# A hybrid network's second layer: ternary weights made by VectorE in pieces, squares added in pairs, and another interleaving of two half-sequences

## The chip, the cores and the metric

One Trainium2 chip, one of its cores. A core has TensorE (PE, matrix products; PEld is its weight load), VectorE (DVE), ScalarE (ACT), GpSimd (POOL) and SyncE (SP, which issues the transfers here). Each engine works through its own instructions in program order; engines wait for each other on semaphores. The metric is the device time of one execution in microseconds (us), less is better. Times in the text are us unless marked.

## The reference, cut to what matters

The network has two layers on a sequence of 1024 tokens with 256 features. The first (attention with rope, a routed block, attention with biases, the routed block again) is not touched. The second is:

```
x = x + L1_attn_a(layernorm(x))     # "r": gates, values = split(h @ W + b); sigmoid, tanh; h_t = g_t * h_(t-1) + v_t
x = x + L1_ffn(layernorm(x))        # "t1": silu(h @ wu) * (h @ wg) @ wd, with ternary weights
x = x + L1_attn_b(layernorm(x))     # "l", "n2", "m": see below
x = x + L1_ffn(layernorm(x))        # "t2": the same ternary weights

def ternary_quant(w):               # 256 x 1024 each
    scale = mean(abs(w)) + 1e-8
    return clip(round(w / scale), -1, 1) * scale

def L1_attn_b(x):
    xn = rmsnorm(x, norm1_w)
    left = gelu(xn @ left_W + left_b)
    right = rg_lru(causal_conv4(xn @ right_W + right_b), ...)   # two gates, exp, sqrt, a scan over the sequence
    x1 = left * right @ out_W + out_b + x
    x1n = rmsnorm(x1, norm2_w)
    return gelu(x1n @ up1_W + up1_b) * (x1n @ up2_W + up2_b) @ down_W + down_b + x1
```

A norm needs for each token the mean over the 256 features and the mean of the squares of what is left after the mean is taken off.

## The kernel before, in words

Features lie on the partitions: x is [128, 2, 1024], two tiles of 128 features (KT = 2) by 1024 tokens. Nearly every product is made of fp32r parts: an operand is split into a rounded "hi" and the rest "lo", and hi·hi, lo·hi and hi·lo are added up in PSUM. A ternary weight needs no lo part, so a block of `up` or `gate` is four matmuls of 128x512 (two hi, two lo), and one step of `down` is four as well; `right`, `left`, `ga`, `gx`, `out`, `up1`, `up2` take six.

The second layer runs in one stage (`layer1`, L1309). The sequence is cut in two halves of 512 tokens, half 0 and half 1, each with four PSUM banks and its own buffers; the second needs the first's last column in the two scans and the convolution. For each engine there are three programs: one that prepares weights (`prep_*`) and one for each half (`half_*`). `by_turns` runs each of them up to its next `yield`, in the order that a string of digits says: 0 for prep, 1 for half 0, 2 for half 1. The four strings (`L1_PE`, `L1_DVE`, `L1_ACT`, `L1_POOL`) are written out, so each engine's order is fixed; when the string is used up, what is left of the programs follows one after the other.

What the prediction speaks of:

- **Norm of a half.** TensorE multiplies x by a constant matrix for the mean (L1552); VectorE subtracts (L1594); ScalarE squares, tile by tile (L1573); TensorE forms the mean of squares as one-column products, four groups of 128 tokens by two tiles (L1562), each an fp32 product that the trace shows as two passes; ScalarE takes the root (L1580); VectorE inverts it and puts it on a diagonal (L1606, L1600); TensorE spreads it over the partitions (L1566); VectorE scales (L1630), ScalarE makes hi (L1587), VectorE lo (L1615). There are ten such variances: r, t1, l, n2, t2 for each half.
- **Ternary weights.** ScalarE sums the absolute values (L1472), TensorE averages over partitions (L1453), VectorE forms the scale and the two bounds (L1506 to L1509), and GpSimd makes the weights in three whole-tensor instructions of 128x2048 for each of up, gate and down: below (L1523), above in place (L1526), above minus below (L1529). After them GpSimd splits the other eight weights into hi and lo (L1540, L1542).
- **The ternary block, t1 and t2.** For f = 0 to 7: up block, sigmoid (L1770), silu on VectorE (L1842), gate block, product (L1846), hi on ScalarE (L1763), lo on GpSimd (L1968), and two steps later the down block (L1661, L1664). The first up, gate and down wait for GpSimd's weights. At the end VectorE adds the result to x (L1850).
- **The l part** adds x1 to u (L1929) when `out` is done; the m part, six steps of f, ends with L1947.
- **r** ends with a scan (L1824) and the sum into x (L1827), VectorE's, for each feature tile.

## Time and profile before

| | |
|---|---|
| median of 3 runs | 1779.75 us (1777.93 to 1782.86) |
| profiled execution | 1778.83 us, of which its span is 1777.6 |
| second layer within the span | 1471 to 1776: 305 us |
| PE busy in those 305 us | 254.2 us, mean granted clock 0.89 |
| DVE / ACT / POOL busy in them | 179.6 / 152.7 / 142.1 us |

In the span, 0 is the start of the profiled program. A timeline row reads: start, duration, engine, line, operation, what it writes and reads, shapes, how many were merged, and in brackets the idle time of the engine just before and what ended it. PEclk, the granted clock, is a share of full speed (2.4 GHz; the lower level is 1.2 GHz, and a stretch between 0.5 and 1 has had both).

### The profile page before, as it was taken

What the parts mean: (1) busy time and instruction counts of PE and PEld (TensorE: products, weight loads), DVE (VectorE), ACT (ScalarE), POOL (GpSimd) and SP (SyncE); (2) the same over time, 40 slices, a digit from 0 to 9 for tenths busy, and PEclk for the clock granted to TensorE, in tenths of its full rate; (3) what the DMA queues carried; (4) which work ended last, traced back from release to release, by engine and by line L of the source; (5) the groups of instructions that cost most, each with busy time, mean ns of one, the idle gap of its engine ahead of it and who ended that gap; (6) DMA issues with size and microseconds to landing.
All of it is one profiled execution on the core that took longest, in us unless ns stands there. A gap on an engine that the chain in (4) does not pass through costs nothing.

```text
span 1777.6 us, 24716 instructions
## 1 busy us (share of the span) xinstructions
PE 1526.5 (86%) x8394; PEld 1259.6 (71%) x8394; DVE 1194.1 (67%) x2825; ACT 966.2 (54%) x2119; POOL 694.4 (39%) x777
## 2 busy tenths in 40 slices
PE   6889897989888887677699999999996777787898
PEld 4768686777777776367488888888884664565676
DVE  4788788888888886453466666666665536577445
ACT  2676767677776776122265555555551235344654
POOL 4446363645545443310242433243322204871223
PEclk8899999999999999787899999999997888898899
DMA  1000000000000000500100000000005004000000
GB/s 65 10 10 7 10 16 1 16 1 16 1 7 1 7 1 1 237 1 0 42 19 13 25 17 20 13 25 19 7 1 237 1 1 166 0 0 1 1 1 24
DMA packets 13936, 46.23 MB, mean 26 GB/s; under 512 B 3058, under 2 KB 3058, under 8 KB 11380
## 3 DMA queue, kind: packets, MB, share of 16 engines
q1 hardware_dynamic: 13812, 44.66, 7.0%
q8 instruction: 68, 1.11, 0.3%
q14 instruction: 56, 0.46, 0.1%
HBM read 43.60 MB, written 1.05 MB: 25 GB/s over the span
## 4 chain that ended last, share of the span: by engine, by line
PE 59%; DVE 18%; ACT 12%; issue 7%; POOL 3%; DMA 0%; DVEq 0%; ACTq 0%; POOLq 0%; SPq 0%
PE ps L140 22%; PE ps L343 13%; PE ps L332 6%; ACT a_prob L362 4%; DVE a_pT_lo L403 4%; PE ps L1651 2%; PE ps L1645 2%; ACT a_pT_hi L395 2%; DVE a_prob L354 2%; ACT a_q L579 1%; PE ps L1155 1%; PE ps L1088 1%; PE ps L213 1%; PE ps L1647 1%; DVE f_r L1283 1%
## 5 line engine op out<-in xcount | busy, mean ns | idle before, releaser
L378 POOL TENSOR_SCALAR a_prob<-a_prob,a_rowinv 128x128 f32<-128x128 f32 (+7 forms) x256 | 192.2, 752 | 307.8 <-DVE a_rowinv L371 307.7
L362 ACT ACTIVATE a_prob<-a_prob,a_negmax 128x128 f32<-128x128 f32 (+7 forms) x256 | 199.0, 777 | 73.8 <-DVE a_negmax L354 72.8
L403 DVE TENSOR_TENSOR a_pT_lo<-ps,a_pT_hi 128x512 fp32r<-128x512 f32 (+3 forms) x384 | 200.9, 551 | 24.4 <-ACT a_pT_hi L395 22.0
L332 PE MATMUL ps<-ident,a_prob 128*128 128x128 f32 x1152 | 177.4, 283 | 41.3 <-DVE a_pT_lo L403 37.0
L378 POOL TENSOR_SCALAR b_prob<-b_prob,b_rowinv 128x128 f32<-128x128 f32 (+7 forms) x128 | 96.2, 751 | 260.6 <-DVE b_rowinv L371 260.6
L354 DVE CUSTOM_DVE_ANT_0 a_prob<-ps,a_mask 128x128 f32<-128x128 f32 (+7 forms) x256 | 191.5, 748 | 2.4 <-PE ps L140 2.3
L395 ACT ACTIVATE a_pT_hi<-ps 128x512 fp32r<-128x512 f32 (+3 forms) x384 | 173.6, 487 | 32.9 <-PE ps L332 29.7
L332 PEld LDWEIGHTS ps<-ident,a_prob 128*128 128x128 f32 x1152 | 135.6, 144 | 65.2 <-POOL a_prob L378 31.7
L140 PE MATMUL ps<-a_k_hi,a_q 128*128 128x512 f32 (+3 forms) x384 | 156.0, 406 | 4.1 <-DVE a_k_lo L628 1.4
L343 PE MATMUL ps<-a_pT_hi,a_v 128*128 128x512 f32 (+3 forms) x384 | 132.3, 352 | 19.5 <-DVE a_pT_lo L403 19.0
L140 PE MATMUL ps<-a_k_lo,a_q 128*128 128x512 f32 (+3 forms) x384 | 131.6, 355 | 0.0
L343 PE MATMUL ps<-a_pT_lo,a_v 128*128 128x512 f32 (+3 forms) x384 | 124.6, 348 | 0.0
L403 DVE TENSOR_TENSOR b_pT_lo<-ps,b_pT_hi 128x128 fp32r<-128x128 f32 (+2 forms) x192 | 99.9, 548 | 2.2 <-ACT b_pT_hi L395 1.5
L362 ACT ACTIVATE b_prob<-b_prob,b_negmax 128x128 f32<-128x128 f32 (+7 forms) x128 | 100.1, 782 | 2.0 <-DVE b_negmax L354 2.0
L343 PEld LDWEIGHTS ps<-a_pT_hi,a_v 128*128 128x128 f32 x384 | 73.1, 190 | 39.5 <-issue 15.9
L1968 POOL TENSOR_TENSOR l_ring_lo<-l_work,l_ring_hi 128x512 fp32r<-128x512 f32 x44 | 57.3, 1307 | 103.8 <-ACT l_ring_hi L1763 103.6
L354 DVE CUSTOM_DVE_ANT_0 b_prob<-ps,b_mask 128x128 f32<-128x128 f32 (+7 forms) x128 | 95.8, 749 | 0.6 <-PE ps L140 0.6
L395 ACT ACTIVATE b_pT_hi<-ps 128x128 fp32r<-128x128 f32 (+2 forms) x192 | 86.3, 488 | 15.0 <-PE ps L332 15.0
L140 PEld LDWEIGHTS ps<-a_k_hi,a_q 128*128 128x128 f32 x384 | 76.3, 199 | 19.6 <-DVE a_negmax L354 11.4
L332 PE MATMUL ps<-ident,b_prob 128*128 128x128 f32 x576 | 84.1, 273 | 2.2 <-POOL b_prob L378 1.7
L636 DVE TENSOR_TENSOR a_o_sum<-ps,a_o_low 64x512 f32<-64x512 f32 x64 | 43.8, 684 | 58.9 <-ACT a_o_low L587 57.9
L140 PEld LDWEIGHTS ps<-a_k_lo,a_q 128*128 128x128 f32 x384 | 76.0, 198 | 6.0
(436 smaller groups left out, 4187.3 us busy)
## 6 DMA issues: line engine op xcount, KB each, us to landing
f_wq<-in_f_wq SPq DMA_DIRECT2D x2, 2048.0 KB, 9.9
f_wo<-in_f_wo SPq DMA_DIRECT2D x2, 2048.0 KB, 18.6
b_w_raw<-in_b_qk SPq DMA_DIRECT2D x16, 256.0 KB, 2.7
a_w_raw<-in_a_w SPq DMA_DIRECT2D x8, 384.0 KB, 3.1
a_o_raw<-in_a_o SPq DMA_DIRECT2D x8, 256.0 KB, 2.6
f_rope<-in_f_rope SPq DMA_DIRECT2D x2, 1024.0 KB, 5.3
f_wk<-in_f_wk SPq DMA_DIRECT2D x2, 1024.0 KB, 11.7
f_wv<-in_f_wv SPq DMA_DIRECT2D x2, 1024.0 KB, 14.4
```

The lines of the kernel that those rows point to most:

```text
L140: t = pe.matmul(out, a, b, start=start and n == 0, stop=stop and n == len(passes) - 1, skip_group_check=True)
L332: t = pe.transpose(g.ps[:, b, j * P:j * P + P], a.prob[:, slot, (j0 + j) * P:(j0 + j + 1) * P], g.ident[:])
L343: t = pe.matmul(out[:, q:HALF], x, y, start=(j == 0 and n == 0), stop=(j == tiles - 1 and n == len(passes) - 1), skip_group_check=True)
L354: dve.tensor_tensor_reduce(a.prob[:, slot, 0:width], g.ps_flat[:, bank * HALF:bank * HALF + width], a.mask[:, N - width:], -1.0, -MASKED, ...
L362: act.activation(prob, prob, ACT.Exp, bias=a.negmax[:, slot:slot + 1], scale=-1.0, accum_out=a.rowsum[:, slot:slot + 1]).then_inc(*g.exped ...
L378: pool.tensor_scalar(prob, prob, a.rowinv[:, slot:slot + 1], 1.0, ALU.mult, ALU.mult).then_inc(*g.normed.mark(a.tag, u))
L395: act.activation(hi, src, ACT.Copy).then_inc(*g.hi.mark(a.tag, u, j0 // 4))
L403: dve.tensor_tensor(lo, src, fr(hi), ALU.subtract).then_inc(*g.lo.mark(a.tag, u, j0 // 4))
L636: dve.tensor_tensor(a.o_sum[ROWS[h % 2], qb], out[0:64], a.o_low[64:128], ALU.add).then_inc(*g.drained.mark(*ev))
L1645: pe.matmul(out, hi[:, k, mm], q.hi[:, k], start=k == 0, stop=False, skip_group_check=True)
L1651: t = pe.matmul(out, hi[:, k, mm], q.lo[:, k], start=False, stop=k == KT - 1, skip_group_check=True)
L1968: pool.tensor_tensor(q.ring_lo[:, f % RING], q.hid[:, f % RING], fr(q.ring_hi[:, f % RING]), ALU.subtract).then_inc(*q.pool.mark(tag, "lo" ...
```

## The change

Three things, all in the second layer.

1. The ternary weights are made by VectorE, in pieces of 1024 columns, two pieces for each weight and two instructions for each piece: below by `tensor_scalar`, then `(raw > bound) - below` in one `scalar_tensor_tensor`. The pieces stand in `prep_dve`, and their places among VectorE's other work are set by the string. GpSimd's three instructions for each weight are gone.
2. ScalarE's two squared tiles are added by VectorE (`half_squares_dve`), and the one-column products are taken over the sum: 4 instead of 8 instructions for a norm. TensorE waits for VectorE there instead of ScalarE. Beside it, the last lo part of each t1, m and t2 is made by VectorE (`half_last_dve`) instead of GpSimd.
3. All four strings are new.

```
-L1_PE = '12121201121211221201...'
+L1_PE = '12121201122101102212...'
 (L1_DVE, L1_ACT and L1_POOL are replaced in the same way)
...
@@ prep_dve
-    for n in range(3):
+    for n, (name, _, _) in enumerate(TERNARY):
...
+        raw, w = l.raw["t", name][:].rearrange(FLAT), l.tern[name][:].rearrange(FLAT)
+        for c in range(2):
+            cc = slice(c * T_E, c * T_E + T_E)
+            dve.wait_ge(*done.at("bounds", n))
+            dve.tensor_scalar(l.below[:, cc], raw[:, cc], s[:, 2:3], None, ALU.is_lt).then_inc(*done.mark("below", n, c))
+            yield
+            dve.wait_ge(*done.at("below", n, c))
+            dve.scalar_tensor_tensor(w[:, cc], raw[:, cc], s[:, 1:2], l.below[:, cc], ALU.is_gt,
+                                     ALU.subtract).then_inc(*done.mark("t", name, c))
+            yield
@@ prep_pool
-    for n, (name, _, _) in enumerate(TERNARY):
-        raw, w = l.raw["t", name][:].rearrange(FLAT), l.tern[name][:].rearrange(FLAT)
...
-        pool.tensor_scalar(l.below[:], raw, l.scale[:, n, 2:3], None, ALU.is_lt).then_inc(*done.mark("below", n))
...
-        pool.tensor_scalar(raw, raw, l.scale[:, n, 1:2], None, ALU.is_gt).then_inc(*done.mark("above", n))
...
-        pool.tensor_tensor(w, raw, l.below[:], ALU.subtract).then_inc(*done.mark("t", name))
-        yield
@@ half_scale_pe
-    pe.wait_ge(*q.act.at(tag, "sq", KT - 1))
+    pe.wait_ge(*q.dve.at(tag, "squares"))
     for j in range(HT):
-        for k in range(KT):
-            t = pe.matmul(q.bank[1][:, j:j + 1], q.sq[:, k, j * P:j * P + P], g.avg[:, 0:1], start=k == 0, stop=k == KT - 1)
+        t = pe.matmul(q.bank[1][:, j:j + 1], q.sq[:, 0, j * P:j * P + P], g.avg[:, 0:1], start=True, stop=True)
+def half_squares_dve(dve, q, tag):
+    dve.wait_ge(*q.act.at(tag, "sq", KT - 1))
+    dve.tensor_tensor(q.sq[:, 0], q.sq[:, 0], q.sq[:, 1], ALU.add).then_inc(*q.dve.mark(tag, "squares"))
+    yield
@@ half_down
-    pe.wait_ge(*q.pool.at(tag, "lo", f))
+    pe.wait_ge(*(q.dve if f == count - 1 else q.pool).at(tag, "ring_lo", f))
@@ half_ternary_pe (and the same for gate and down)
-                pe.wait_ge(*g.prep_pool.at("t", "up"))
+                pe.wait_ge(*g.prep_dve.at("t", "up", 1))
+def half_last_dve(dve, q, tag, f):
+
+    dve.wait_ge(*q.act.at(tag, "ring", f))
+    dve.tensor_tensor(q.ring_lo[:, f % RING], q.hid[:, f % RING], fr(q.ring_hi[:, f % RING]),
+                      ALU.subtract).then_inc(*q.dve.mark(tag, "ring_lo", f))
```

`half_squares_dve` is called in each norm after the mean is taken off (for n2 after x1), `half_last_dve` before the last additions to x; `half_hidden_pool` runs over `count - 1` steps.

How the instructions move is told at three places. In the rows, `half0_act` and the like are semaphores of one half and engine, `prep_*` those of the weights' programs.

First VectorE, before, from the scale of `up` to the centring of half 0 in t1: the lo parts of half 1, the scans and sums of r (L1824, L1827).

```order
L1506 TENSOR_SCALAR l_scale<-ps 128x1 [waits prep_pe]
L1508 TENSOR_SCALAR l_scale<-l_scale 128x1 [waits prep_dve]
L1509 TENSOR_SCALAR l_scale<-l_scale 128x1
L1615 TENSOR_TENSOR l_h_lo<-l_h,l_h_hi 128x512 [waits half1_act] x2
L1824 SCALAR_TENSOR_TENSOR l_left<-l_work 128x512 [waits half0_act]
L1827 TENSOR_TENSOR x<-x,l_left 128x512 [waits half0_dve]
L1829 COPY l_r_last<-l_left 128x1
L1824 SCALAR_TENSOR_TENSOR l_left<-l_work,l_r_last 128x512 [waits half1_act,half0_dve]
L1827 TENSOR_TENSOR x<-x,l_left 128x512 [waits half1_dve]
L1824 SCALAR_TENSOR_TENSOR l_left<-l_work 128x512 [waits half0_act]
```

The same place of the change (L1515 and L1518 are the pieces, L1827 and L1830 scan and sum):

```order
L1515 TENSOR_SCALAR l_below<-l_t_raw_up,l_scale 128x1024 [waits prep_dve]
L1518 SCALAR_TENSOR_TENSOR l_t_up<-l_t_raw_up,l_scale,l_below 128x1024 [waits prep_dve]
L1515 TENSOR_SCALAR l_below<-l_t_raw_up,l_scale 128x1024 [waits prep_dve]
L1827 SCALAR_TENSOR_TENSOR l_left<-l_work 128x512 [waits half0_act]
L1830 TENSOR_TENSOR x<-x,l_left 128x512 [waits half0_dve]
L1832 COPY l_r_last<-l_left 128x1
L1518 SCALAR_TENSOR_TENSOR l_t_up<-l_t_raw_up,l_scale,l_below 128x1024 [waits prep_dve]
L1506 TENSOR_SCALAR l_scale<-ps 128x1 [waits prep_pe]
L1508 TENSOR_SCALAR l_scale<-l_scale 128x1 [waits prep_dve]
L1509 TENSOR_SCALAR l_scale<-l_scale 128x1
L1515 TENSOR_SCALAR l_below<-l_t_raw_gate,l_scale 128x1024 [waits prep_dve]
L1827 SCALAR_TENSOR_TENSOR l_left<-l_work 128x512 [waits half0_act]
```

Pieces of the weights now stand between the scans of half 0, and half 0's second scan comes ahead of half 1's first.

Second TensorE at the start of t1, before: the first blocks of up and gate of the two halves stand in turn.

```order
L1645 MATMUL ps<-l_h_hi,l_t_up 128x512 [waits half0_act,prep_pool]
L1645 MATMUL ps<-l_h_hi,l_t_up 128x512 [waits half0_act]
L1651 MATMUL ps<-l_h_lo,l_t_up 128x512 [waits half0_dve] x2
L1566 MATMUL ps<-l_diag,ones 128x512 [waits half1_dve]
L1645 MATMUL ps<-l_h_hi,l_t_up 128x512 [waits half1_act,prep_pool]
L1645 MATMUL ps<-l_h_hi,l_t_up 128x512 [waits half1_act]
L1651 MATMUL ps<-l_h_lo,l_t_up 128x512 [waits half1_dve] x2
L1645 MATMUL ps<-l_h_hi,l_t_gate 128x512 [waits prep_pool]
```

And in the change (L1648 and L1654 are the hi and lo products, L1558 the one-column ones):

```order
L1648 MATMUL ps<-l_h_hi,l_t_up 128x512 [waits half0_act,prep_dve]
L1648 MATMUL ps<-l_h_hi,l_t_up 128x512 [waits half0_act]
L1654 MATMUL ps<-l_h_lo,l_t_up 128x512 [waits half0_dve] x2
L1558 MATMUL ps<-avg,l_sq 128x1 [waits half1_dve]
L1558 MATMUL ps<-avg,l_sq 128x1 x3
L1648 MATMUL ps<-l_h_hi,l_t_gate 128x512 [waits prep_dve]
L1648 MATMUL ps<-l_h_hi,l_t_gate 128x512
L1654 MATMUL ps<-l_h_lo,l_t_gate 128x512 x2
L1648 MATMUL ps<-l_h_hi,l_t_up 128x512 [waits half0_dve]
```

Half 0 goes ahead alone there: half 1's first up block comes after half 0's second down block. When TensorE has issued half 0's last down block of t1, 84 of half 1's 96 matmuls of t1 are still to come; before it was 56.

Third GpSimd after the split of r's weights, as one piece of the difference (L1537 and L1539 are L1540 and L1542 of before):

```order
-L1523 TENSOR_SCALAR l_below<-l_t_raw_up,l_scale 128x2048
-L1526 TENSOR_SCALAR l_t_raw_up<-l_t_raw_up,l_scale 128x2048
-L1529 TENSOR_TENSOR l_t_up<-l_t_raw_up,l_below 128x2048
-L1523 TENSOR_SCALAR l_below<-l_t_raw_gate,l_scale 128x2048
-L1526 TENSOR_SCALAR l_t_raw_gate<-l_t_raw_gate,l_scale 128x2048
-L1529 TENSOR_TENSOR l_t_gate<-l_t_raw_gate,l_below 128x2048
-L1523 TENSOR_SCALAR l_below<-l_t_raw_down,l_scale 128x2048
-L1526 TENSOR_SCALAR l_t_raw_down<-l_t_raw_down,l_scale 128x2048
-L1968 TENSOR_TENSOR l_ring_lo<-l_work,l_ring_hi 128x512
-L1529 TENSOR_TENSOR l_t_down<-l_t_raw_down,l_below 128x2048
```

The splits of left, right and ga follow r's at once, ahead of the first lo part of half 0.

## Rows read from the trace of the kernel before

**Rows 1.** The page: the span, and busy time of each engine.
```profile
span 1777.6 us, 24716 instructions
PE 1526.5 (86%) x8394; PEld 1259.6 (71%) x8394; DVE 1194.1 (67%) x2825; ACT 966.2 (54%) x2119; POOL 694.4 (39%) x777
```
**Rows 2.** Stretches of the second layer: length, busy time of each engine, granted clock, DMA.
```profile
1495.00:1515.00 20.00, 10.20 (x36) 6.42 (x35) 14.16 (x11) 6.53 (x9) 9.49 (x2) 0.74 0.00 1
1515.00:1532.00 17.00, 10.19 (x35) 5.55 (x34) 10.07 (x20) 6.61 (x10) 15.80 (x4) 0.74 0.00 0
1532.00:1547.50 15.50, 11.59 (x40) 8.56 (x38) 7.33 (x10) 6.21 (x10) 15.41 (x5) 0.83 0.00 0
...
sum 305.00, PE 254.16 PEld 184.56 DVE 179.56 ACT 152.71 POOL 142.12; mean PE 23.11 PEld 16.78 DVE 16.32 ACT 13.88 POOL 12.92
```
**Rows 3.** Waits of PE from 1471 to 1776: us in total, times, longest.
```profile
PE ps L1552 <- DVE l_r_last L1829: 9.5, 1, 9.5
PE ps L1661 <- POOL l_t_down L1529: 3.5, 1, 3.5
PE ps L1645 <- POOL l_t_gate L1529: 3.3, 1, 3.3
```
**Rows 4.** Timeline of POOL: the ternary weights, and a later split.
```profile
1487.65 6.32 POOL L1523 TENSOR_SCALAR l_below<-l_t_raw_up,l_scale 128x2048 bf16<-128x2048 f32 x1 [8.85 <-DVE l_scale L1509]
1494.07 5.44 POOL L1526 TENSOR_SCALAR l_t_raw_up<-l_t_raw_up,l_scale 128x2048 f32<-128x2048 f32 x1
1499.60 4.97 POOL L1529 TENSOR_TENSOR l_t_up<-l_t_raw_up,l_below 128x2048 fp32r<-128x2048 f32 x1
...
1543.34 4.07 POOL L1529 TENSOR_TENSOR l_t_down<-l_t_raw_down,l_below 128x2048 fp32r<-128x2048 f32 x1
...
1579.34 3.45 POOL L1542 TENSOR_TENSOR l_up_lo<-l_raw_up,l_up_hi 128x1536 fp32r<-128x1536 f32 x1
```
**Rows 5.** Timeline of DVE beside those POOL instructions.
```profile
1494.21 4.65 DVE L1824 TENSOR_TENSOR_SCAN l_left<-l_work,l_r_last 128x512 f32<-128x512 f32 x1
...
1499.51 1.22 DVE L1824 TENSOR_TENSOR_SCAN l_left<-l_work 128x512 f32<-128x512 f32 x1
1500.76 4.36 DVE L1827 TENSOR_TENSOR x<-x,l_left 128x512 f32<-128x512 f32 x1
...
1580.03 2.77 DVE L1867 TENSOR_TENSOR l_inv<-l_inv 128x4 f32<-128x4 f32 x1
```
**Rows 6.** DVE's groups by form: busy time, mean ns of one.
```profile
L1248 DVE TENSOR_TENSOR f_diag<-f_s,ident 128x1024 f32<-128x1024 f32 x2 | 2.5, 1226 | 0.1
...
L1908 DVE SCALAR_TENSOR_TENSOR l_work<-l_work,l_right 128x512 f32<-128x512 f32 x4 | 2.8, 694 | 0.1
...
L1051 DVE TENSOR_SCALAR f_probT<-f_s,f_s_col 128x896 bf16<-128x896 f32 x2 | 1.3, 674 | 0.0
```
**Rows 7.** Timeline of PE at full clock: a block, and the one-column products of a norm.
```profile
1736.24 1.84 PE L1562 MATMUL ps<-avg,l_sq 128*128 128x1 f32 x16
1737.94 0.71 PE L1645 MATMUL ps<-l_h_hi,l_t_gate 128*128 128x512 f32 x2
...
1765.04 0.62 PE L1645 MATMUL ps<-l_h_hi,l_t_up 128*128 128x512 f32 x2
1765.50 0.63 PE L1651 MATMUL ps<-l_h_lo,l_t_up 128*128 128x512 f32 x2
1765.97 0.63 PE L1645 MATMUL ps<-l_h_hi,l_t_gate 128*128 128x512 f32 x2
```
**Rows 8.** Timeline of DVE: the additions that end t1, l and m.
```profile
1569.26 1.41 DVE L1850 SCALAR_TENSOR_TENSOR x<-ps,l_scale,x 128x512 f32<-128x512 f32 x2 [1.52 <-PE ps L1664]
...
1610.96 1.41 DVE L1850 SCALAR_TENSOR_TENSOR x<-ps,l_scale,x 128x512 f32<-128x512 f32 x2 [7.53 <-PE ps L1664]
...
1628.16 0.75 DVE L1929 SCALAR_TENSOR_TENSOR l_u<-ps,l_bias,l_u 128x512 f32<-128x512 f32 x1 [1.81 <-PE ps L1651]
...
1685.73 0.75 DVE L1929 SCALAR_TENSOR_TENSOR l_u<-ps,l_bias,l_u 128x512 f32<-128x512 f32 x1 [1.81 <-PE ps L1651]
1687.08 1.56 DVE L1947 SCALAR_TENSOR_TENSOR x<-ps,l_bias,x 128x512 f32<-128x512 f32 x2 [0.60 <-PE ps L1664]
```
**Rows 9.** The chain of waits at the end: start, duration, what.
```profile
1767.70 0.76 DVE l_work L1846
...
1770.51 0.76 DVE l_work L1846
1771.27 0.02 issue
1771.29 0.64 ACT l_ring_hi L1763
1771.94 0.07 issue
1772.01 1.27 POOL l_ring_lo L1968
1773.28 0.04 issue
```

More of the change, by code:

```diff
@@ L1344 @@
 HT = HALF // P
[L1345 to L1348 removed]
+L1_PE = '1212120112210110221211211121111112112111111111211121222122222111221111111222222221122121121112212221212222111111112212112122122122222222221122112121111211121111211122122121222222221212222222222'
+L1_DVE = '10121202012112112202000100012110012012211110200112001121122211111122111112112111222211121111111111112221122111111112211212212211112122212222222222221221222212222222112112221211212111222111212112121122211211222211222222122122122122122222'
+L1_ACT = '1120201201122110121201212121121211112112211111121112211222121211111112112111221212112111221112121221122222212222121212212211222112122121222222211211111221121112212122212222122222222'
+L1_POOL = '0000100110112112022212121011211212122222211111212212222'
 def by_turns(g, e, order, *programs):
@@ L1517, in prep_pool @@
     yield
-    for n, (name, _, _) in enumerate(TERNARY):
-        raw, w = l.raw["t", name][:].rearrange(FLAT), l.tern[name][:].rearrange(FLAT)
-        pool.wait_ge(*g.prep_dve.at("bounds", n))
-        if n:
-            pool.wait_ge(*done.at("t", TERNARY[n - 1][0]))
-        pool.tensor_scalar(l.below[:], raw, l.scale[:, n, 2:3], None, ALU.is_lt).then_inc(*done.mark("below", n))
-        yield
-        pool.wait_ge(*done.at("below", n))
-        pool.tensor_scalar(raw, raw, l.scale[:, n, 1:2], None, ALU.is_gt).then_inc(*done.mark("above", n))
-        yield
-        pool.wait_ge(*done.at("above", n))
-        pool.tensor_tensor(w, raw, l.below[:], ALU.subtract).then_inc(*done.mark("t", name))
-        yield
     for name, _, _ in L_W:
@@ L1626, in half_norm_dve @@
     yield from half_centre_dve(dve, q, tag)
+    yield from half_squares_dve(dve, q, tag)
     yield from half_inverse_dve(g, dve, q, tag)
@@ L1696, in half_ternary_pe @@
             if f == 0:
-                pe.wait_ge(*g.prep_pool.at("t", "gate"))
+                pe.wait_ge(*g.prep_dve.at("t", "gate", 1))
             else:
@@ L1703, in half_ternary_pe @@
             if f == 2:
-                pe.wait_ge(*g.prep_pool.at("t", "down"))
+                pe.wait_ge(*g.prep_dve.at("t", "down", 1))
             half_down(pe, q, down, f - 2, TE_T, tag)
@@ L1847, in half_ternary_dve @@
         yield
+    half_last_dve(dve, q, tag, TE_T - 1)
+    yield
     for m in range(KT):
@@ L1856, in half_lru_dve @@
     yield from half_centre_dve(dve, q, "l")
+    yield from half_squares_dve(dve, q, "l")
     dve.wait_ge(*act.at("l", "std"))
@@ L1930, in half_lru_dve @@
         yield
+    yield from half_squares_dve(dve, q, "n2")
     yield from half_inverse_dve(g, dve, q, "n2")
@@ L1943, in half_lru_dve @@
         yield
+    half_last_dve(dve, q, "m", RF_T - 1)
+    yield
     for m in range(KT):
@@ L1965, in half_hidden_pool @@
 def half_hidden_pool(pool, q, tag, count):
-    for f in range(count):
+    for f in range(count - 1):
         pool.wait_ge(*q.act.at(tag, "ring", f))
         pool.tensor_tensor(q.ring_lo[:, f % RING], q.hid[:, f % RING], fr(q.ring_hi[:, f % RING]),
-                           ALU.subtract).then_inc(*q.pool.mark(tag, "lo", f))
+                           ALU.subtract).then_inc(*q.pool.mark(tag, "ring_lo", f))
         yield
```

4 lines of the change are left out of this document (removed).

## The prediction

> **What bounds the kernel now.** I read the page first: 1777.6 us of span, PE busy 86% of it [rows 1]. The change touches the second layer alone, so next the stretches of that layer: 305 us, in which PE is busy 254.2 us, DVE 179.6 and POOL 142.1 [rows 2]. PE is the busiest engine there, but 51 us it stands idle, and much of its busy time is at a reduced clock. Three stretches in a row are the poorest: from 1495 to 1547.5 PE is busy 10.2 of 20, 10.2 of 17 and 11.6 of 15.5 us, at granted clocks of 0.74, 0.74 and 0.83, which lie between its two levels, 1.2 and 2.4 GHz [rows 2]. In the last two of them POOL is busy 15.8 of 17 and 15.4 of 15.5 us [rows 2]: there POOL is the bound. The waits of PE say on what: 9.5 us on VectorE's end of r (L1829), 3.5 and 3.3 us on POOL's ternary weights for down and gate [rows 3]. The timeline of POOL shows the chain: 6.32, 5.44 and 4.97 us for up, and so on until the last of nine, for down, ends at 1543.34 + 4.07 = 1547.4 [rows 4].
>
> The 9.5 us wait on VectorE has the same root. A scan of 128x512 takes 1.22 us when nothing disturbs it, but the one that begins at 1494.21, just behind POOL's L1526 at 1494.07, takes 4.65; and the sum L1827, which begins at 1500.76 under POOL's L1529 (1499.60 + 4.97 = 1504.57), takes 4.36 and ends at 1505.12 [rows 4, 5]. An instruction over 512 columns with two inputs in SBUF takes 0.69 when free [rows 6]. So VectorE lost 3.4 + 3.7 = 7.1 us there to POOL, on the path of half 0 into t1.
>
> This is what the Trainium skill says in SBUF — State Buffer, "SBUF: two separate sides": VectorE and GpSimd share a pair of ports as an exclusive lock, and an instruction of VectorE with two SBUF inputs waits for the whole instruction of GpSimd that came first. This trace agrees in the main: L1827 ends 0.55 us behind POOL's L1529 and L1867 with POOL's L1542, but the scan ended 0.65 us before L1526 did [rows 4, 5].
>
> **The change part by part.**
>
> *Ternary weights.* Removed: POOL's nine instructions, 6.32 + 5.44 + 4.97 for up and about 15 each for the others, some 46 us [rows 4]. Added on VectorE: six pieces. Below is a one-input compare to bf16; the same form over 896 columns takes 0.674 [rows 6], so 0.77 at 1024. The other has two SBUF inputs; the nearest row is a tensor_tensor over 1024 columns, 1.226 [rows 6], and L1908 shows that the scalar form costs no more than the plain one. A piece is 2.0 us, six are 12.0. Bounds: 4 us less if the bf16 input sped up the second instruction to the first one's rate (6 times 0.46 makes 2.8), and 12 us more if each of the six met a POOL split: the long one takes 3.45 [rows 4], half of it waited for is 1.7, and 0.3 for each piece's hand-overs comes to it. I take 12.0, as most splits are short.
>
> Now I walk the start with these durations. VectorE's work for the r norm comes some 2 us later than before, since the second half's add waits for ScalarE behind the softplus; so the scale of up is known at about 1489 and up's first piece ends at 1491.5. The scans then stand between pieces: half 0's first at 1493 to 1494.2, its second, behind up's second piece and gate's first compare, ends at 1498.6, the sum at 1499.2. That was 1505.1. Mean, centring, squares, add, one-column products, root, diagonal and its product (the same steps as before, with one gate piece in the way) bring the first up block of half 0 to about 1512.5; before it was 1519.5. Gate's weights are complete at 1508, so its first gate block follows at once, where it was held until 1531.0. From there half 0 runs alone, limited by its own chain. The end of the trace gives the period of such a chain: L1846 of one f begins at 1767.70, that of the next at 1770.51, 2.81 apart [rows 9]. At the lower clock and with the down pieces and half 1's norm on VectorE's queue (4.0 + 0.9 + 2.7 us) the first two steps take 4.5 each, the other six 3.0 to 3.3. Its last addition to x comes at about 1547; it was at 1569.26 + 1.41 = 1570.7 [rows 8]. That is 24 us for half 0.
>
> *But half 1 pays for part of it.* When half 0 ends t1, 84 matmuls of half 1's t1 are left instead of 56. A block of four takes 1765.97 − 1765.04 = 0.93 us at full clock, 0.233 for each matmul [rows 7]. So I take the next landmark where both orders have done the same: half 0's residual of m (L1947, ends 1687.08 + 1.56 = 1688.6 [rows 8]), with half 1's x1 just before it.
> By the road of TensorE: before, from 1570.7 to 1688.6 are 118 us, in which 284 matmuls (66 us) and 14.7 us of norm products fall (two means, four variances, six inverses, near 1.7, 1.7 and 0.9 each; the 1.70 is from row L1562 to the next start [rows 7]); 37 us are lost. In the change 312 matmuls are 73 us, the norms 11.3; with the same loss that is 121, so 1668.
> By the road of half 1's chain: half 0 goes from the end of t1 (1570.7) to its x1 (1628.16 + 0.75 = 1628.9) in 58.2 us [rows 8]. In it L1867, over 4 columns, took 2.77 under POOL's 3.45 of L1542 [rows 4, 5], and the instructions after it met the next splits: about 4 us that go, since most splits are now made earlier. So x1 of half 0 at 1601, and half 1's end of t1, which stands just behind it, at 1606 (before 1612.4). From there half 1 took 1686.5 − 1612.4 = 74.1 us to its x1; half 0 took 58.2. That gives 1664 to 1680.
> I take 1668, where the first road ends and within the second: 20.4 us less than 1688.6.
>
> *Squares in pairs.* Each norm saves half of 1.70 us on TensorE, 0.85, and adds a 128x512 add with two SBUF inputs, 0.69 [rows 6], and a hand-over of some 0.05. Where the norm is on the path that nets 0.1; where TensorE is the bound it is 0.85. Four variances are in the walk, four in the sum above (3.4 us), two come after it: 1.7 us, in a stretch where PE is full. Bounds: nothing, or 0.85 each.
>
> *The last lo part.* At the end of the kernel POOL's 1.27 us is on the chain [rows 9]; VectorE's is 0.69. That is 0.6 us. Elsewhere other blocks hide it.
>
> *The strings.* After the landmark the order is nearly what it was; ScalarE changes its table three more times in the layer, and I give that nothing, because half of the stretch is PE-bound.
>
> Sum: 20.4 + 1.7 + 0.6 = 22.7 us off the profiled execution's 1778.8, so 1756. The median of before, 1779.75, is 0.9 above that execution; I forecast 1757.
>
> **The rivals.**
>
> *Half 1's chain decides* (13 in 100). Its l part takes the full 74.1 us again, since half 0's m part now runs wholly beside it. For: half 0's x1, behind which m begins, comes 5 us before half 1 enters l, where it came 16.5 us after [rows 8]. Against: TensorE has the room. Landmark at 1680: 6.5 + 2.3 off, 1770.
>
> *TensorE's idle time shrinks as well* (15 in 100). Half 0's l part has 84 matmuls of half 1 beside it, 6.6 us more, and where PE idles less its clock stays up: the stretches above at 0.74 would have been a quarter shorter. If 10 of the 37 lost us go too, 1746.
>
> *The lock moves with the weights* (6 in 100). POOL's splits of left, right, ga, gx, out and up1 now run beside VectorE's pieces, scans and adds, all of two SBUF inputs, and half 0's lo parts queue behind a split of 5 us. If the pieces pay the 12 us upper bound and each of them is ahead of a silu, half 0 ends t1 at 1560 and the landmark is near 1679: 1768. By the skill's rule this would happen wherever the two start together; POOL has 46 us less to hold the lock with, which is why I give it little.
>
> *Slower: half 1 comes too late* (3 in 100). Before, after half 0's t1, half 1's last four steps of f took 1612.4 − 1570.7 = 41.7 us, 10.4 each, stretched by half 0's l part. If seven steps are stretched so, half 1 ends t1 at 1547 + 73 = 1620, 8 us later than before, and everything behind it too: 1785 to 1788. It decides from 1612.4 plus the 5 us of a measurable loss. Against it: the last steps stand close behind half 0's x1.
>
> *The walk is right but the saved time is given back* (4 in 100), for instance by the mean of half 1, which waits on its scan ahead of half 0's inverse: within 5 us of 1779.75.
>
> **How the numbers follow.** The forecast has 59 in 100, with a range of its own from 1749 to 1765: the two roads' ends. Half 1's chain, more room and the lock bring it to 1741 and 1771, which leaves out the two last cases and a little on the fast side. A difference of 0.3%, 5.3 us, is about what a measurement of this kernel tells from no change. Faster by more than that: 0.59 + 0.13 + 0.15 + 0.06 = 0.93; the same 0.04; slower 0.03.
>
> **What would show it right or wrong.** Right: six instructions of 0.75 and six of 1.23 us on VectorE, no waits of PE on ternary weights; half 0's end of t1 near 1547, x1 of half 1 near 1667, the end of the layer near 1753; DVE scans of r at 1.22. The rule of the pieces is wrong if they take 3 us or more. The whole is wrong if the end of half 0's t1 is early and half 1's x1 not: then the gain was only moved from one half to the other. If PE's busy time falls by more than the 8.5 us of the one-column products, the clock gave it.

## The result, and the profile after

| | median, us | ratio to before, 95% interval |
|---|---|---|
| before | 1778.84 | 1 |
| changed | 1757.84 (1756.06 to 1758.47) | 0.9878 [0.9858, 0.9899] |

The forecast was 1757. The page of the changed kernel, first its length and then the busy times:

```profile
span 1756.0 us, 24570 instructions
PE 1514.6 (86%) x8314; PEld 1248.7 (71%) x8314; DVE 1213.1 (69%) x2853; ACT 968.6 (55%) x2122; POOL 645.1 (37%) x762
```

Against [rows 1] TensorE has 11.9 us less to do, and yet the span fell by 21.6: TensorE also stood idle for 9.7 us less. The waits of TensorE in the second layer, over 2 us (total, times, longest):

```profile
PE ps L1558 <- DVE l_sq L1596: 10.0, 6, 3.7
PE ps L1648 <- ACT l_h_hi L1583: 9.4, 9, 1.9
PE ps L1648 <- DVE l_work L1845: 5.4, 3, 3.3
PE ps L1648 <- ACT l_work L1814: 3.4, 4, 2.5
PE ps L1549 <- DVE l_r_last L1832: 3.1, 1, 3.1
PE ps L1562 <- DVE l_diag L1602: 2.9, 3, 1.4
```

No ternary weight is waited for any more; L1549's 3.1 answers to the 9.5 of [rows 3]. In place of these waits, TensorE now waits 10.0 us for VectorE's new additions of squares, L1596. The landmarks on VectorE's timeline (start, duration): half 0 ends t1, half 1 ends t1, half 1's x1 (L1942), half 0 ends m, half 1 ends t2.

```profile
1549.23 1.41 DVE L1855 SCALAR_TENSOR_TENSOR x<-ps,l_scale,x 128x512 f32<-128x512 f32 x2 [0.17 <-PE ps L1667]
...
1607.55 1.40 DVE L1855 SCALAR_TENSOR_TENSOR x<-ps,l_scale,x 128x512 f32<-128x512 f32 x2
...
1663.17 0.75 DVE L1942 SCALAR_TENSOR_TENSOR l_u<-ps,l_bias,l_u 128x512 f32<-128x512 f32 x1 [0.66 <-PE ps L1654]
...
1670.65 1.44 DVE L1963 SCALAR_TENSOR_TENSOR x<-ps,l_bias,x 128x512 f32<-128x512 f32 x2 [1.14 <-PE ps L1667]
...
1752.52 1.41 DVE L1855 SCALAR_TENSOR_TENSOR x<-ps,l_scale,x 128x512 f32<-128x512 f32 x2 [0.83 <-PE ps L1667]
```

The ends of these (1550.6, 1609.0, 1663.9, 1672.1 and 1753.9) answer to 1570.7, 1612.4, 1686.5 and 1688.6 in [rows 8] and to 1775.5 at the end of the kernel before:

```profile
1774.09 1.41 DVE L1850 SCALAR_TENSOR_TENSOR x<-ps,l_scale,x 128x512 f32<-128x512 f32 x2 [2.83 <-PE ps L1664]
```

Half 0's t1 gained 20.1 us, half 1's only 3.4, half 1's x1 22.6, half 0's m (the landmark of the prediction) 16.5, and the end 21.6.

### The profile page after: what moved, and what is told of

Same layout as the page of the kernel before. It is cut to its first block, busy times and chain, and to the rows that moved or that the text cites. A ratio compares the mean times of both kernels' runs of the same rounds, so it can differ in the third digit from the quotient of the medians.

```text
span 1756.0 us, 24570 instructions
## 1 busy us (share of the span) xinstructions
PE 1514.6 (86%) x8314; PEld 1248.7 (71%) x8314; DVE 1213.1 (69%) x2853; ACT 968.6 (55%) x2122; POOL 645.1 (37%) x762
## 4 chain that ended last, share of the span: by engine, by line
PE 59%; DVE 19%; ACT 13%; issue 7%; POOL 1%; DMA 0%; DVEq 0%; ACTq 0%; POOLq 0%; SPq 0%
PE ps L140 22%; PE ps L343 13%; PE ps L332 6%; ACT a_prob L362 4%; DVE a_pT_lo L403 4%; ACT a_pT_hi L395 2%; PE ps L1648 2%; PE ps L1654 2%; DVE a_prob L354 2%; ACT a_q L579 1%; PE ps L1155 1%; PE ps L1088 1%; PE ps L213 1%; DVE f_r L1283 1%; DVE a_q L626 1%
## 5 line engine op out<-in xcount | busy, mean ns | idle before, releaser
L343 PE MATMUL ps<-a_pT_hi,a_v 128*128 128x512 f32 (+3 forms) x384 | 132.2, 351 | 19.4 <-DVE a_pT_lo L403 19.0
L343 PE MATMUL ps<-a_pT_lo,a_v 128*128 128x512 f32 (+3 forms) x384 | 124.7, 348 | 0.0
L1984 POOL TENSOR_TENSOR l_ring_lo<-l_work,l_ring_hi 128x512 fp32r<-128x512 f32 x38 | 49.6, 1314 | 138.3 <-ACT l_ring_hi L1766 138.3
L140 PEld LDWEIGHTS ps<-a_k_hi,a_q 128*128 128x128 f32 x384 | 76.3, 199 | 19.6 <-DVE a_negmax L354 11.5
## 6 DMA issues: line engine op xcount, KB each, us to landing
f_wk<-in_f_wk SPq DMA_DIRECT2D x2, 1024.0 KB, 11.9
```

The costliest lines, as they stand in the source:

```text
L140: t = pe.matmul(out, a, b, start=start and n == 0, stop=stop and n == len(passes) - 1, skip_group_check=True)
L343: t = pe.matmul(out[:, q:HALF], x, y, start=(j == 0 and n == 0), stop=(j == tiles - 1 and n == len(passes) - 1), skip_group_check=True)
L1984: pool.tensor_tensor(q.ring_lo[:, f % RING], q.hid[:, f % RING], fr(q.ring_hi[:, f % RING]), ALU.subtract).then_inc(*q.pool.mark(tag, "rin ...
```

## The layer in four stretches

The table below is what the experiments are read by. It is worked out from the timeline of each profiled execution, counted from the first matmul of the second layer (L1549 or L1552). That is needed because the first layer, the same in all kernels, did not end at the same time. A row is one execution, each figure rounded by itself; the ratios are those of all runs. Of two kernels, with the pieces alone and with the last third interleaved anew, these are the starts:

```profile
1475.15 3.67 PE L1549 MATMUL ps<-x,avg 128*128 128x512 f32 x8 [0.83 <-PE ps L1170]
```

```profile
1468.54 3.67 PE L1549 MATMUL ps<-x,avg 128*128 128x512 f32 x8 [0.83 <-PE ps L1170]
```

They lie 6.6 us apart, more than most effects here. So a landmark's time on the clock can't be compared between two executions, unless both layers start together, as those of before and of the changed kernel do (1471.1).

| kernel | to t1 end, half 0 | to t1 end, half 1 | to m end, half 0 | to the end | layer | ratio of times |
|---|---|---|---|---|---|---|
| before | 99.6 | 41.7 | 76.3 | 86.9 | 304.4 | 1 |
| pieces alone | 93.4 | 41.5 | 76.0 | 86.8 | 297.8 | 0.9959 [0.9938, 0.9981] |
| new rows alone | 91.3 | 61.9 | 60.9 | 82.5 | 296.6 | 0.9959 [0.9944, 0.9973] |
| pieces + new rows | 80.9 | 55.6 | 60.9 | 82.5 | 279.9 | 0.9869 [0.9849, 0.9890] |
| changed (those + pairs) | 79.5 | 58.3 | 63.1 | 81.8 | 282.8 | 0.9878 [0.9858, 0.9899] |
| new rows + pairs, no pieces | 92.6 | 65.7 | 62.8 | 81.8 | 302.9 | 0.9982 [0.9970, 0.9994] |
| changed, another first norm | 80.6 | 56.4 | 59.9 | 81.8 | 278.8 | 0.9865 [0.9850, 0.9880] |
| the same without pairs | 78.3 | 56.9 | 62.8 | 82.4 | 280.4 | 0.9882 [0.9868, 0.9896] |
| the same, pairs in the last two norms | 78.2 | 55.1 | 60.4 | 81.8 | 275.6 | 0.9853 [0.9835, 0.9871] |

## Experiments: the parts one by one

"New rows" are the interleaving of the changed kernel, with the last lower half on VectorE.

**The pieces alone.** Before, with

```
+ (prep_dve, behind each scale)  is_lt to bf16, then is_gt and subtract, 2 x 128x1024
- (prep_pool)                    below, above, t: 3 x 128x2048 for each weight
  VectorE's row: four steps of 0 behind each scale; the other rows as before
```

> The kernel before, with one part of the change: VectorE makes the ternary weights in pieces of 128x1024, each of the three sets right behind its scale; GpSimd no longer makes them. Sums of squares, last lower half and interleaving stay as before (the three scales' places in VectorE's row too). Theory A (the gain is that the first up block and the first down block of half 0 stop waiting for GpSimd, and that the half that waited 24 us less then starts everything earlier): the first up block starts near 1512 where it was 1519.5, the 3.5 and 3.3 us waits of TensorE for ternary weights are gone, half 0 ends t1 near 1555 or earlier where it was 1570.7; the interleaving of before holds part back, so about 1764 us, 1757 to 1771. Rival B (the new interleaving carries the gain, the weights' engine is a side matter): over 1774. Rival C (fewer one-column products carry it): over 1774 too.

It took 1775.99 us (1767.29 to 1777.16) against 1781.36 of before, ratio 0.9959. Theory A asked for 1757 to 1771 and fell; rivals B and C both asked for this number, and the next runs tell them apart. The waits for ternary weights did go, but only 6.2 us in the first stretch came of it. TensorE's timeline shows what came next:

```profile
1516.91 0.28 PE L1453 MATMUL ps<-l_part,l_avg 128*128 128x1 f32 x2
1522.56 3.57 PE L1559 MATMUL ps<-avg,l_sq 128*128 128x1 f32 x16 [5.37 <-ACT l_sq L1570]
1525.99 1.20 PE L1642 MATMUL ps<-l_h_hi,l_t_up 128*128 128x512 f32 x2
```

L1559 are half 1's one-column products, which stand in TensorE's row ahead of half 0's first up block (L1642). They wait 5.37 us for half 1's squares. VectorE shows why:

```profile
1516.59 0.76 DVE L1515 TENSOR_SCALAR l_below<-l_t_raw_gate,l_scale 128x1024 bf16<-128x1024 f32 x1
1517.38 1.28 DVE L1518 SCALAR_TENSOR_TENSOR l_t_gate<-l_t_raw_gate,l_scale,l_below 128x1024 fp32r<-128x1024 f32 x1
...
1519.36 1.28 DVE L1518 SCALAR_TENSOR_TENSOR l_t_gate<-l_t_raw_gate,l_scale,l_below 128x1024 fp32r<-128x1024 f32 x1
1520.56 1.28 DVE L1591 TENSOR_TENSOR l_h<-x,ps 128x512 f32<-128x512 f32 x2
```

Gate's four instructions run ahead of half 1's centring (L1591). The up weights are there, but the row lets half 0 go no faster than half 1: its first up block comes 50.8 us into the layer, where before it came at 48.4. The pieces stood right behind each scale here; other places for them in the old rows were not tried, so the 6.2 us hold for these places.

**The new rows alone.** The changed rows of TensorE, ScalarE and VectorE, with the weights on GpSimd and 8 products:

```
- dve: pieces, squares          + pool: below, above, t (nine steps)
  GpSimd's row: '0000000001011001102110202020212121...'
```

> The new interleaving alone: ternary weights on GpSimd as before (GpSimd's splits between the lower halves again), 8 one-column products, no additions of squares; TensorE's, ScalarE's and VectorE's rows are the new ones, with the last lower half on VectorE. It completes the square of which before (1780.8 in the last call), the pieces alone (1776.0) and pieces with rows (1757.65) are three corners. Theory (early weights and rows that let half 0 run ahead are worth little apart and 20 us together, since TensorE then neither waits for weights nor for half 1): 1776 us, 1772 to 1780. Rival (they add up): 1781 less 18, 1763. With the additions of squares this corner took 1777.7.

1771.32 us against 1779.13, ratio 0.9959. So apart each part is worth 0.41%; if they multiplied, both would give 0.9918, and they give 0.9869. The missing 0.5% is some 9 us (give or take 6, by the three intervals) that neither has without the other. The theory has the sign and the kind right, though the rows alone did better than the 1776 expected and fell just under its range. In the first stretch the pieces are worth 6.2 us under the old rows and 10.4 under the new ones; 6.3 more come in the second.

**The changed kernel with the weights back on GpSimd.**

```
- dve: pieces    + pool: below, above, t    (additions of squares stay)
```

> The changed kernel, with the ternary weights back on GpSimd in the three whole passes each of before; GpSimd's row begins as before (its splits of left, right, ga, gx, out and the others between the lower halves again), VectorE's row is that of the changed kernel without the pieces. Squares in pairs, the last lower half on VectorE and the interleaving of TensorE, VectorE and ScalarE stay as changed. Theory A: the gain is lost, and an order made for early weights sits on late ones: the first up block near 1519, TensorE's waits for ternary weights back; 1778 us, 1770 to 1788. Rival B (the interleaving carries the gain): under 1764. If the parts add up: 1757.8 plus what the pieces alone gained.

1777.71 us, ratio 0.9982 [0.9970, 0.9994]: theory A's number and not rival B's, nor the 1763 of parts that add up. TensorE waits for the weights again:

```profile
PE ps L1561 <- DVE l_sq L1599: 12.7, 6, 3.2
...
PE ps L1667 <- POOL l_t_down L1529: 5.8, 1, 5.8
PE ps L1552 <- DVE x L1833: 4.4, 1, 4.4
```

**The changed kernel without the pairs.**

```
-    pe.wait_ge(*q.dve.at(tag, "squares"))            (4 products)
+    pe.wait_ge(*q.act.at(tag, "sq", KT - 1))         (8 products)
-    yield from half_squares_dve(...)                 in r, t1, l, n2, t2
```

> The changed kernel, with 8 one-column products in each norm again and without VectorE's ten additions; all else as changed. Theory A: TensorE's busy time up by about 8.5 us, of which what is saved on VectorE takes back nearly all up to the landmark at 1672 and not behind it, where half 1 alone feeds TensorE: 1759.5 us, 1757 to 1762. Rival C (the squares carry a good part of the gain): 1766 or more. Rival (the additions only cost): 1754 or less.

1757.65 us against the changed kernel's 1757.84, so no worth of the pairs as placed in it can be told. Theory A had this, within its range. The cause shows in two groups of the changed kernel (busy time and mean ns of one, then the idle time ahead):

```profile
L1558 PE MATMUL ps<-avg,l_sq 128*128 128x1 f32 x80 | 12.8, 281 | 10.2 <-DVE l_sq L1596 10.0
```

```profile
L1596 DVE TENSOR_TENSOR l_sq<-l_sq 128x512 f32<-128x512 f32 x10 | 10.9, 1092 | 3.4 <-ACT l_sq L1569 3.4
```

Before had 160 of these products in 19.4 us with 6.7 us of waits ahead of them; now 80 take 12.8 with 10.0. The busy time saved is 6.6 us, the waits are 3.3 longer, and an addition takes 1.09 us on average where I had written 0.69. The worst one:

```profile
1601.75 1.49 POOL L1537 TENSOR_SCALAR l_down_hi<-l_raw_down 128x1536 fp32r<-128x1536 f32 x1
1603.32 3.76 POOL L1539 TENSOR_TENSOR l_down_lo<-l_raw_down,l_down_hi 128x1536 fp32r<-128x1536 f32 x1
```

```profile
1603.70 3.93 DVE L1596 TENSOR_TENSOR l_sq<-l_sq 128x512 f32<-128x512 f32 x1
1607.55 1.40 DVE L1855 SCALAR_TENSOR_TENSOR x<-ps,l_scale,x 128x512 f32<-128x512 f32 x2
```

Half 0's addition begins 0.38 us behind GpSimd's lower half of down, and ends 0.55 behind its end; half 1's end of t1 stands behind it. That is the 58.3 against 55.6 us of the second stretch in this execution. This is again the exclusive lock of the Trainium skill's page SBUF — State Buffer, "SBUF: two separate sides", and here the trace agrees.

## Experiments: where an addition stands

**Before, with the pairs alone.**

```
+ half_squares_dve in every norm, 4 products
  VectorE's row: a step ahead of each reciprocal or of what needs TensorE behind the products
```

> The kernel before, with one part of the change: VectorE adds the two blocks of squares, and TensorE does 4 one-column products in a norm instead of 8. Everything else as before; the ten additions are put into VectorE's row ahead of whatever needs TensorE behind the products. Theory A (0.85 us saved on TensorE at each of ten norms against 0.75 us of addition on the same path): TensorE's busy time falls by about 8.5 us, the time stays within 3 us of before: 1778 us, 1774 to 1782. Rival C (the 8.5 us of TensorE are on the path): 1770. Rival: each norm gets longer by an addition and its handover, 1.0 us at each of the eight norms behind 1500: 1784 or more.

1805.45 us against 1781.36, ratio 1.0131 [1.0114, 1.0149], 24 us slower: the last rival's side, and far in it. The waits of TensorE for the additions are 31.5 us, in nine places. The first norm:

```profile
1482.73 3.57 PE L1561 MATMUL ps<-avg,l_sq 128*128 128x1 f32 x16 [5.43 <-DVE l_sq L1599]
```

I had put these two additions behind the softplus instructions, which wait for ScalarE.

**The same with other places.**

```
  the r additions ahead of softplus; the others one or two steps behind the centring or the sums
```

> The kernel before with squares in pairs and half as many one-column products, as in the run with the squares alone (1805.5), but with the ten additions elsewhere in VectorE's row: in the r norm both ahead of the five softplus instructions, the others within one or two instructions behind the centring or the sums whose squares they add, instead of just ahead of the reciprocal. If the 24 us were the places (an addition behind an instruction that waits holds up TensorE's products): 1779 us, 1775 to 1783. If a sum in pairs is slower on this path wherever it stands: 1795 or more.

1790.24 us, ratio 1.0059 [1.0044, 1.0074]. Places alone are worth 15 us. Still, 9 us are left over before, so neither expectation holds: I found no places in the old rows where the pairs cost nothing. The waits for additions are 17.8 us, and the two of the first norm stall on the shared lock again:

```profile
1477.63 3.81 DVE L1599 TENSOR_TENSOR l_sq<-l_sq 128x512 f32<-128x512 f32 x2
```

## Experiments: which rows matter

**New rows in the last third only**, and **new rows from half 0's first up block on**; both have the pieces, the last lower half on VectorE and 8 products.

```
  rows_last:     rows of before up to TensorE's step 113, new ones behind
  rows_from_t1:  rows of before up to TensorE's step 23, new ones behind (GpSimd's new from its second step)
```

> Ternary pieces and the last lower half of each product on VectorE, squares as before (8 one-column products). The rows of all four engines are those of before up to the end of half 0's first up product of its last hidden block in the gated MLP (TensorE's step 113, about 1680 us), and those of the changed kernel from there to the end: only the last third is interleaved anew. In the runs so far the time from half 0's m residual to the end was 86.9 us with the rows of before and 81.8 to 82.5 with the new ones, whoever made the weights. If that is the rows' doing: 1771 us (the 1776.0 of the kernel with the ternary pieces alone less 5), 1768 to 1773. If it is the shorter way there that does it: 1775 to 1777.

> Ternary pieces and the last lower half of each product on VectorE, squares as before. The rows are those of before up to TensorE's first up block of half 0 (step 23, about 1515 us), and the new ones from there on. With the run before it and the changed kernel without the squares in pairs (1757.65) it splits the 18 us between the pieces alone (1776.0) and that kernel into three stretches. Theory A2 (the rows of before tie half 0's ternary block by block to half 1's, which early weights can't help; the new ones let half 0 run ahead): nearly all of the middle's gain is here: 1760 us, 1757 to 1764. Rival (the stalls of VectorE beside GpSimd's splits in the r stage decide, that is the first stretch): 1766 or more.

1772.46 and 1764.70 us, ratios 0.9957 [0.9942, 0.9971] and 0.9912 [0.9894, 0.9930]. The last stretch is 82.5 us in both, and 81.8 to 82.5 in every kernel with new rows there, as against 86.8 and 86.9 with the old ones. Part of these 4.4 us is only where the landmark falls. Here is the last stretch before, and with pieces and new rows (window, length, TensorE's busy time and matmul records first):

```profile
1688.60:1775.50 86.90, 82.31 (x354) 62.54 (x353) 45.70 (x67) 45.45 (x65) 28.39 (x22) 1.00 0.02 7
```

```profile
1670.20:1752.60 82.40, 80.12 (x344) 61.05 (x342) 45.97 (x67) 41.86 (x62) 24.84 (x19) 1.00 0.02 7
```

The new rows put half 0's m residual later beside half 1's work: ten matmul records, 2.2 us of TensorE's busy time, now lie ahead of it. The rest is idle time of TensorE, 4.6 us and now 2.3. In the kernel with new rows in the last third only, the third stretch pays for what the last one gains (79.1 us, and 76.0 with the pieces alone): half 0's m residual comes 6.4 us behind half 1's x1, and with the pieces alone 2.1. From half 1's x1 to the end the two take 88.9 and 89.0 us. So in the layer as a whole no gain of new rows in the last third alone can be told, and the times say the same (0.9957 and 0.9959): the expected 1771 came (1772.46), but not as its reason had it. From half 0's t1 to half 1's too this kernel was 3.2 us longer than the one with the pieces alone, under the same rows. It also has the last lower half on VectorE, and its granted clock there was 0.85 where that one had 0.92; which of the two it was stays open.

The second lies between the two expectations. Its last three stretches are those of pieces with new rows (55.7, 60.9, 82.5), while the first is 87.2 against 80.9. So the 18 us between the pieces alone (1776.0) and the full rows (1757.65) are some 11 behind the first up block and 7 ahead of it (8 and 8 by the ratios), the 5.4 us wait for half 1's products among them. Theory A2 underrated that first part.

## Experiments: a better version

**The first norm in another order**, with pairs and then without:

```
ScalarE:  sq 1, sq 1, sq 2, sq 2, std 1, std 2, softplus, ln, hi 1, hi 1, abs up, ...
VectorE:  both additions and both inverses ahead of the softplus steps
```

> The changed kernel with another order in the first norm: on ScalarE all four squares and both square roots ahead of the softplus and the logarithm, which then stand ahead of half 0's upper halves, and the first sum of magnitudes behind them; on VectorE both additions of squares and both inverses ahead of the softplus instructions. The wait of 3.7 us of TensorE for the second sum of squares goes, and with it two table loads (1.28 us each) between squares and root. Half 0's r residual ends about 3 us earlier (1501 instead of 1504), and what follows, if VectorE (40 of 50 us busy there) keeps pace: 1755 us, 1753 to 1757. Rival: VectorE's pieces are what half 0 waits for by then, and nothing moves: 1757.8.

> The kernel with the new order in the first norm (1755.99), now with 8 one-column products and no additions of squares. The two kernels with the old order of the first norm took 1757.84 with and 1757.65 without the pairs, so the pairs are worth nothing and this gives 1756 us, 1754 to 1757.5. If the pairs cost in VectorE's idle cover what the profile of the one without them shows (its second layer was 279.9 us long against 282.8 with them): 1753.

1755.99 us, ratio 0.9865 [0.9850, 0.9880], and 1758.56, ratio 0.9882 [0.9868, 0.9896]. The 1504 of the expectation was half 1's sum, misread: half 0's r residual ends 30.9 us into the layer in the changed kernel, and 32.0 in this one, so it is not earlier (without the pairs 29.8 against 31.0). The time of the first has the expected sign, but its interval overlaps the changed kernel's; the second is no faster than with the old order (1757.65). So this order is worth nothing that can be told.

The first of the two says more on the pairs. It has all ten of them, and from half 0's t1 on its rows are the changed kernel's; yet its second and third stretch took 56.4 and 59.9 us where that one's took 58.3 and 63.1. The add that had lost 3.2 us to GpSimd's lower half of down now begins 1.5 us ahead of it, and takes half as long:

```profile
1608.50 1.96 DVE L1596 TENSOR_TENSOR l_sq<-l_sq 128x512 f32<-128x512 f32 x1
```

and the third stretch ran at a granted clock of 0.97 in place of 0.89 (compare the rows further down):

```profile
1611.80:1671.60 59.80, 50.57 (x197) 35.58 (x196) 42.49 (x62) 34.85 (x49) 15.51 (x11) 0.97 0.00 0
```

So those 5 us are no price of the pairs: they differ between two kernels with the same pairs. Against the kernels without pairs at the same 0.97 its third stretch is 1.0 us shorter, and its last one 0.6 us shorter than without pairs. Its first stretch is 2.3 us longer than the same without pairs; with the old first norm the pairs had made it 1.4 us shorter (79.5 against 80.9).

**Pairs only in the last two norms of each half.**

```
+ PAIRED = ("n2", "t2")      4 products and an addition there, 8 and none elsewhere
```

> As the run before it, but with squares in pairs in the two last norms of each half (the gated MLP's and the second ternary's), where TensorE is the bound: its clock is 1.00 there and it hardly waits. Theory (a saved product is worth its time only where TensorE is the bound): four norms at 0.85 us saved, the additions hidden beside TensorE's other work: 2 us under the run before it, 1754 us, 1752 to 1756. Rival (the wait for the addition eats it there too): the same as the run before.

1751.11 us (1750.43 to 1759.25), ratio 0.9853 [0.9835, 0.9871]: the lowest of all, 1.5% under before and with its median under the changed kernel's, though its interval overlaps a little with those of the changed kernel and of the one without pairs. The sign is the theory's, the size more than that. Of the 7.4 us to the kernel without pairs only some 1 us can be seen to be theirs: already at half 0's x1, ahead of the first pair, its profiled execution was 2.9 us earlier in the layer. The third stretch of the two (window, length, TensorE's busy time first, its granted clock third from the end), without pairs and with them at the end:

```profile
1607.50:1670.30 62.80, 57.25 (x220) 42.41 (x220) 40.25 (x62) 35.05 (x49) 13.73 (x11) 0.89 0.00 1
```

```profile
1605.10:1665.60 60.50, 51.36 (x205) 36.57 (x204) 42.05 (x62) 34.94 (x49) 15.64 (x11) 0.97 0.00 1
```

And of pieces with new rows, whose rows in this stretch are those of the first:

```profile
1609.30:1670.20 60.90, 53.12 (x219) 38.27 (x220) 40.74 (x61) 35.05 (x49) 15.73 (x11) 0.97 0.00 1
```

The same matmuls were 57.3 or 53.1 us of busy time at the two granted clocks, and the stretch was 1.9 us longer at the lower one, under the same rows. Against the execution at the same 0.97 the pairs give 0.4 us there, and 0.6 in the last stretch.

**GpSimd's splits later.** As the kernel with 8 products and the new first norm; in GpSimd's row a split now follows each lower half.

```
  '0000100110112112...'  ->  '0101010101020112...'
```

> As the run with 8 products and the new order of the first norm, but GpSimd splits left, right, ga, gx, out and up1 one at a time between the lower halves of half 0's first ternary instead of in a row during the r stage. Theory (VectorE stalls beside them wherever they stand; in the r stage it is half 0's norm and pieces that stall, 7 us from 1486 on): the r residual ends 2 to 4 us earlier in the layer, and the stalls come back within the ternary, where VectorE has some slack: 1755 us, 1752 to 1758. Rival (a lower half that waits behind a split of 2 to 3 us holds up the down block): over 1759.

1759.98 us, ratio 0.9891 [0.9873, 0.9908]: above the theory's range and in the rival's (over 1759), by 1 us, while the interval overlaps that of the kernel it is to be compared with (1758.56). In the first 31.8 us of the layer VectorE was busy 3.3 us less, and yet half 0's r residual came at 29.8 and its first up block at 41.6 us in both kernels: its stalls beside the splits in the r stage were hidden. The rival's mechanism came in the first ternary:

```profile
PE ps L1658 <- POOL l_ring_lo L1976: 5.0, 1, 5.0
```

The first stretch grew from 78.3 to 85.2 us. Of these 7.0 the next two gave 4.7 back (to 54.1 and 60.9, at granted clocks of 0.97 in place of 0.88 and 0.89), so the whole time says little of the splits.

## Why the prediction was right, point by point

- **Ternary pieces: right in kind, 2.5 us small.** Twelve instructions, 14.5 us of them against 12.0. Free ones took 0.75 and 1.27 to 1.29. Two compares took 1.78 and 1.85, beside a split (ga) and a lower half of GpSimd, and one second instruction 1.51, beside the split of gx; that is the whole difference. (The lower bound, 4 us less, stands beside a working of 2.8.)

```profile
1492.13 1.78 DVE L1515 TENSOR_SCALAR l_below<-l_t_raw_up,l_scale 128x1024 bf16<-128x1024 f32 x1
1493.94 1.29 DVE L1518 SCALAR_TENSOR_TENSOR l_t_up<-l_t_raw_up,l_scale,l_below 128x1024 fp32r<-128x1024 f32 x1
```

- **The walk to the end of t1: right, up to 3.6 us short.** Half 0's r residual came at 1502.0 (1499.2 forecast), its first up block at 1515.3 (1512.5), the end of t1 at 1550.6 (1547). The scale of up came at 1491, 2 us late, since VectorE's lower halves L1617 stalled beside GpSimd's splits of left and right; with the 1.0 us of the first compare above these are the 2.8, carried on to the first up block.
- **"Half 1 pays for part of it": right, the landmark by luck in part.** Half 0's x1 1602.5 (1601), half 1's t1 1609.0 (1606), the landmark 1672.1 (1668). From half 0's t1 to it 121.5 us passed, and TensorE's road had said 121. But the kernel with all the pairs and another first norm took 116.3 for the same road, and that without pairs 116.5, where the road's own working, without its 3.4 us for them, would say 124.7. So "with the same loss" did not hold in general. (The norm products of that road add up to 15.6 us by the prices given, not 14.7; the same sum is taken off and put back, so its end doesn't move by it.)
- **The step that failed: a landmark "where both orders have done the same", with half 1's x1 "just before it", and "after the landmark the order is nearly what it was".** Half 1's x1 was to come near 1667 and came at 1663.9, 22.6 us earlier than before; the landmark came 8.2 us behind it, where before it came 2.2 behind. The new rows had put ten more matmul records ahead of the landmark, 2.2 us of TensorE's time. For the stretch behind it I gave 2.3 us, 1.7 for the pairs and 0.6 for the last lower half; it gave 5.1. Of these some 2.2 are that moved work, 0.6 the pairs (82.5 to 81.8), 0.6 the last lower half (TensorE's wait for it fell from 1.6 to 1.0), and the rest, under 2 us, other idle time gone. So the 3.9 us too much ahead of the landmark and 2.8 too little behind it are for the most part one error counted twice, and the total came out closer than its parts.
- **Pairs: mis-sized.** 3.4 us in TensorE's road and 1.7 behind it were credited; taking the pairs out cost nothing measurable, and where they show in the profiles it is by some 1.0 and 0.6 us in the last two stretches. The ten norms saved 6.6 us of products and not 8.5, an addition cost 1.09 us and not 0.69, and 0.05 for the handover was a wait of up to 3.7.
- **The cause as told was half of it.** I put the gain down to the weights' engine, working it out for the new rows throughout. The square of runs says that under the old rows it would have been 5 to 7 us (medians, ratio).
- **The clock.** I wrote that more than 8.5 us off TensorE's busy time would be the clock's. 11.9 went, 6.6 of them by the products. The cleaner pair is before and pieces with new rows, both with 990 matmuls in the layer: 254.2 and 247.1 us, at granted clocks of 0.89 and 0.94. These 7 us came with the shorter idle times; that the one causes the other was not tried by itself, and the same 990 took 251.8 us at 0.91 in the kernel without pairs and with another first norm. The stretches at 0.74 would not have been "a quarter shorter" at the full clock either: only TensorE's busy part of them, 10.2 of 20 and of 17 us, could shrink.
- **The rivals.** Half 1's chain did not hold its 74.1 us: from its t1 to its x1 it took 55. The rival of more room (1746) did not come about in the changed kernel; in two other executions there are 5 us of it (116.5 without the pairs, 116.3 with all of them and another first norm, instead of 121.5 from half 0's t1 to the landmark), both at a higher granted clock in the third stretch. The lock did move with the weights, but took 2.5 us from the pieces and not 12.

## What to carry to other kernels

Where each engine runs through a fixed row of two interleaved streams, a faster step is worth little until the rows let its stream run ahead: measure the step and the order both alone and together before crediting either. An addition that saves matmul time is a new handover and, with two SBUF inputs, one more instruction that can stall beside GpSimd; put it only where TensorE is the bound (here the profiles say so by 1 to 2 us, and the times don't tell it), and not behind an instruction that waits. Count landmarks from the start of the part that changed, compare stretches at the same granted clock, and when the order changes, count the matmuls on each side of a landmark before calling a shorter stretch a gain.

## What the runs showed of the hardware

- A compare with one input in SBUF, f32 to bf16, stalls beside GpSimd too: 0.75 us free, 1.78 and 1.85 beside its instructions. I had looked for this only in instructions with two SBUF inputs.
- The same matmuls under the same rows ran, in the third stretch, at a granted clock of 0.89 in one kernel and 0.97 in four, 57.3 against 53.0 to 53.1 us of busy time. With the pairs in every norm it was 0.89 in two (54.8 and 54.9 us) and 0.97 in one (50.6).
- The first layer, the same code everywhere, ended between 1468.5 and 1475.2 us in the fourteen profiled executions.
